# Graph-network kernel on one core: last layer's bias per node, 64 target nodes to a group, a third gate buffer

## What is computed

```python
def _mlp(x, w1, b1, w2, b2, w3, b3):
    x = relu(x @ w1.T + b1)
    x = relu(x @ w2.T + b2)
    return x @ w3.T + b3
def _prop_once(node_states, f_idx, t_idx, edge_features, ...):
    edge_inputs = concatenate([node_states[f_idx], node_states[t_idx], edge_features], axis=1)
    return segment_sum(_mlp(edge_inputs, ...), t_idx)
agg  = _prop_once(x, edge_attr, src, dst, ...)
agg += _prop_once(x, edge_attr, dst, src, ...)
s1 = _gru(x, agg); s2 = _gru(agg, s1); s3 = _gru(s1, s2)
x = layernorm(x + s3)
```

## Time and profile before

| | us |
|---|---|
| median of 3 runs | 2416.49 (2416.43 to 2416.96) |
| profiled execution, its own time | 2414.69 |
| its span in the trace | 2412.9 |
| PE busy | 2290.2 (95%) |
| DVE busy | 1702.4 (71%) |
| ACT busy | 1220.0 (51%) |
| POOL busy | 1356.8 (56%) |

### The profile page before, as it was taken

How to read it: one execution, slowest core, us unless ns; L and a number is a source line. 1 busy time by engine, 2 the same in 40 slices (tenths; PEclk the granted TensorE clock), 3 DMA queues, 4 the chain that set the end, 5 groups by cost and what they waited for, 6 DMA issues and landing times. The chain is left out here.

```text
span 2412.9 us, 42177 instructions
## 1 busy us (share of the span) xinstructions
PE 2290.2 (95%) x12735; PEld 1908.4 (79%) x12735; DVE 1702.4 (71%) x3628; ACT 1220.0 (51%) x2106; POOL 1356.8 (56%) x846
## 2 busy tenths in 40 slices
PE   5999999999999999999999999999999769699997
PEld 3888888888888888888888888888888645488886
DVE  7877878878778788788788788788787456602114
ACT  4555555555556665565565565565555314211112
POOL 2676777777767776776777677777767400000000
PEclk9999999999999999999999999999999979899998
DMA  4456555445555545555545555545555450295863
GB/s 159 83 112 121 98 98 107 89 84 108 96 100 106 92 81 107 94 101 106 93 80 106 95 105 100 97 85 98 100 106 93 60 217 1 107 383 228 348 276 150
DMA packets 233808, 293.73 MB, mean 122 GB/s; under 512 B 125755, under 2 KB 191294, under 8 KB 225228
## 3 DMA queue, kind: packets, MB, share of 16 engines
q1 hardware_dynamic: 160457, 237.91, 35.3%
q0 software_dynamic: 73216, 54.58, 17.7%
HBM read 219.35 MB, written 73.05 MB: 121 GB/s over the span
## 5 line engine op out<-in xcount | busy, mean ns | idle before, releaser
L446 POOL DMA_INDIRECT sums<-outb,target x416 | 684.3, 1645 | 417.3 <-ACT outb L609 167.0
L439 POOL DMA_INDIRECT xg<-in_x,gidx x416 | 667.8, 1605 | 159.5 <-issue 140.2
L591 ACT ACTIVATE h<-ebank,b2c 128x512 f32<-128x512 f32 x416 | 287.3, 691 | 346.6 <-PE ebank L1152 333.2
L1163 PEld LDWEIGHTS ebank<-w3t,h 128*128 128x128 f32 x3328 | 404.1, 192 | 13.8
L1163 PE MATMUL ebank<-w3t,h 128*128 128x128 f32 x3328 | 404.9, 275 | 0.0
L1152 PE MATMUL ebank<-h1h,w2h 128*128 128x512 f32 x832 | 365.3, 439 | 3.9 <-DVE h1l L806 3.9
L1152 PE MATMUL ebank<-h1h,w2l 128*128 128x512 f32 x832 | 329.9, 397 | 0.0
L1152 PE MATMUL ebank<-h1l,w2h 128*128 128x512 f32 x832 | 328.6, 395 | 0.0
L585 ACT ACTIVATE h1h<-hpre 128x512 fp32r<-128x512 f32 x416 | 237.8, 622 | 93.0 <-DVE hpre L801 92.0
L806 DVE SCALAR_TENSOR_TENSOR h1l<-hpre,h1h 128x512 fp32r<-128x512 f32 x416 | 258.4, 678 | 0.0
L1138 PE MATMUL ebank<-sdh,w1h 128*128 128x512 f32 x624 | 247.4, 396 | 2.1 <-DVE sdl L827 1.5
(11 more groups left out here) (254 smaller groups left out, 4000.0 us busy)
## 6 DMA issues: line engine op xcount, KB each, us to landing
ring<-adj SPq DMA_DIRECT2D x54, 1568.0 KB, 8.0
rowb<-along SPq DMA_DIRECT2D x104, 512.0 KB
adj<-band SPq DMA_DIRECT2D x25, 1500.0 KB, 14.6
ef<-in_edge_attr SPq DMA_DIRECT2D x103, 256.0 KB, 2.7
stay<-adj SPq DMA_DIRECT2D x6, 1568.0 KB, 14.4
xg<-in_x,gidx POOLq DMA_INDIRECT x416
sums<-outb,target POOLq DMA_INDIRECT x416
xw<-in_x SPq DMA_DIRECT2D x104, 40.0 KB
```

The lines of the kernel that those rows point to most:

```text
L439: pool.indirect_dma_start(out=to, out_offset=None, in_=a["x"], in_offset=bass.IndirectOffsetOnAxis(ap=ids, axis=0)).then_inc(s_x[par], 16)
L446: pool.indirect_dma_start(out=tables[k % 2], out_offset=bass.IndirectOffsetOnAxis(ap=target[par][:, 1, k:k + 1], axis=0), in_=outb[par][:, ...
L591: nc.scalar.activation(h2[:, way, f, :], bank[6 + f][:, :], ACT.Relu, bias=b2c[:, f:f + 1]).then_inc(s_h2, 1)
L1163: last = nc.tensor.matmul(bank[6 + way][:, t * P:(t + 1) * P], h2[:, way, k, t * P:(t + 1) * P], w3t[:, k, :], start=False, stop=(t == K - ...
```

## The change

**Bias.** `third` loses its two bias products in the path that these inputs take. In place of them the number of edges into each node and out of each is counted, and at the end of the edge stage seven products (2 rows of b3 by 448 nodes' degrees) and seven DVE additions add b3 times the two degrees to `aggt`. The in-degrees come from an accumulated output of `hot` (for each of the window's nodes, the number of the group's edges into it). For the out-degrees the count has 25 more columns, a one-hot of the edge's target block, and DVE adds these columns to `outdeg` in `count_pairs`. At the end both pass through DRAM (two stores, four loads, issued by ACT) to become rows.

**Window.** SPAN is 64 and BACK 10, and `aggt` becomes a slice of a wider `aggw`, so that no window is cut off at the ends; WIN is 19, which makes room for the 25 columns (25 * 19 + 25 = 500).

**Gates** has three buffers, and ACT waits for the cell three back. Beside that, POOL's zero fill at the start of the sum stage waits for the copies into `zt`.

```diff
-WIN = 20
+WIN = 19
 WIDE = NB * WIN
+WIDER = WIDE + NB
-BACK = 16
-SPAN = 80
+BACK = 10
+SPAN = 64
...
@@ ACT, edge stage, the last turn
+                    if win and not ahead:
+                        degrees_away()
                     results(g)
                     sums(g, par, early)
+                    if win and not ahead:
+                        degrees_back()
...
@@ DVE, edge stage
                     nc.vector.tensor_scalar(hot[0:SPAN, :], rowb[par][0:SPAN, 0, :], wnode[0:SPAN, bass.ds(g, 1)], None,
-                                            ALU.is_equal).then_inc(s_hot, 1)
+                                            ALU.is_equal, ALU.add,
+                                            accum_out=indeg[0:SPAN, bass.ds(g + BEFORE, 1)]).then_inc(s_hot, 1)
...
+                    step(nc.vector.tensor_scalar(ints, flat(colkey), 3450.0, None, ALU.mult))
+                    step(nc.vector.tensor_scalar(ints, ints, 16, None, ALU.logical_shift_right))
+                    step(nc.vector.tensor_copy(flat(blkkey), ints))
...
                     for t in range(K):
                         nc.vector.tensor_scalar(rowhot[:, t, :], spots[:, 0:P], of(rowkey, t), None, ALU.is_equal)
-                        last = nc.vector.tensor_scalar(colhot[:, t, :], spots[:, 0:WIDE], of(colkey, t), None, ALU.is_equal)
-                    last.then_inc(s_ah, 1)
+                        nc.vector.tensor_scalar(colhot[:, t, 0:WIDE], spots[:, 0:WIDE], of(colkey, t), None, ALU.is_equal)
+                    nc.vector.tensor_tensor(
+                        colhot[:, :, WIDE:WIDER], column[:, 0:NB].unsqueeze(1).broadcast_to([P, K, NB]),
+                        blkkey[:, bass.ds(g, 1), :].rearrange("p g k -> p (g k)").unsqueeze(2).broadcast_to([P, K, NB]),
+                        ALU.is_equal).then_inc(s_ah, 1)
...
+                    nc.vector.tensor_tensor(outdeg[:, half, :], outdeg[:, half, :], bank[4 + half][:, WIDE:WIDER], ALU.add)
                     nc.vector.tensor_tensor(part, part, bank[4 + half][:, 0:WIDE].rearrange("p (b c) -> p b c", c=WIN),
                                             ALU.add).then_inc(s_acc, 1)
...
+                for n, bk in enumerate((3, 4, 5, 6, 7, 2, 0)):
+                    dve.wait_ge(s_degp, n + 1)
...
+                    nc.vector.tensor_tensor(aggt[:, cols], aggt[:, cols], bank[bk][:, 0:CH], ALU.add).then_inc(s_whole, 1)
...
@@ PE, edge stage
-            def third(g):
+            def third(g, bias=False):
                 pe.wait_ge(s_h2, g * 4 + 4)
                 for way in range(2):
-                    nc.tensor.matmul(bank[6 + way][:, :], ones_r[:, :], b3hl[:, :, :].rearrange("p k d -> p (k d)"),
-                                     start=True, stop=False)
+                    if bias:
+                        nc.tensor.matmul(bank[6 + way][:, :], ones_r[:, :], b3hl[:, :, :].rearrange("p k d -> p (k d)"),
+                                         start=True, stop=False)
...
+                def last_bias():
+
+                    pe.wait_ge(s_degrow, 4 * 16)
+                    pe.wait_ge(s_deg, 2)
+                    pe.wait_ge(s_es, G * 2)
+                    for n, bk in enumerate((3, 4, 5, 6, 7, 2, 0)):
+                        if bk == 0:
+                            pe.wait_ge(s_agg, G)
+                        nc.tensor.matmul(bank[bk][:, 0:CH], b3r[0:2, :], (degree_lo if n < 4 else degree_hi)[0:2, n % 4 * CH:(n % 4 + 1) * CH],
+                                         start=True, stop=True).then_inc(s_degp, 1)
...
@@ GRU stage
-        gates = sb("gates", [P, 2, 2, CH])
+        gates = sb("gates", [P, 3, 2, CH])
...
-                if seq >= 2:
-                    act.wait_ge(s_cell, seq - 1)
+                if seq >= 3:
+                    act.wait_ge(s_cell, seq - 2)
...
@@ POOL, sum stage
+            pool.wait_ge(s_tc, NGR)
             nc.gpsimd.memset(xn[:, :, :], 0.0).then_inc(s_zero, 1)
```

More of the change, by code:

```diff
@@ L58 @@
 PACE = 30
-BACK = 16
-SPAN = 80
-NB_A = 16
+BACK = 10
+SPAN = 64
+NB_A = 19
 AHEAD = 10
-assert G == 4 * ITERS and WIDE <= 512
+assert G == 4 * ITERS and WIDER <= 512
 ADUMMY = NR * AW
@@ L66 @@
 CH = 448
+QS = -(-(N + BACK) // PACE)
+BEFORE = (SPAN - 1) // PACE
+WIDTH_A = (G - 1) * PACE + SPAN
+assert WIDTH_A >= BACK + AW and WIDTH_A % NB_A == 0
 CHUNKS = [(c, min(CH, N - c)) for c in range(0, N, CH)]
@@ L169, in edge_stage @@
         whalf = sd_flat[:, 2 * H:4 * H].rearrange("p (f j c) -> p f j c", f=HB, j=2)
+        degree_lo = hpre[:, :, :, :].rearrange("p f w e -> p (f w e)")
+        degree_hi = sdh[:, :, :].bitcast(fp32).rearrange("p j e -> p (j e)")
         at = lambda t, lo, shape: t[:, lo:lo + int(np.prod(shape))]
@@ L966, in turn, with degrees_out @@
                         places(g + 1, 1 - par, early=early == 2)
+                    if not ahead:
+                        degrees_out()
                     deliver(g)
+                def degrees_out():
+                    dve.wait_ge(s_acc, G * 2)
+                    nc.vector.tensor_tensor(outdeg[:, 2, :], outdeg[:, 0, :], outdeg[:, 1, :], ALU.add).then_inc(s_deg, 1)
+                    dve.wait_ge(s_degT, 1)
+                    nc.vector.tensor_copy(indegs[0:QS, :], bank[2][0:QS, 0:PACE]).then_inc(s_deg, 1)
                 onehot(0, 0, 0)
@@ L1164, in third @@
                                                     h2[:, way, k, t * P:(t + 1) * P], w3t[:, k, :],
-                                                    start=False, stop=(t == K - 1 and k == HB - 1))
+                                                    start=not bias and k == 0,
+                                                    stop=(k == HB - 1 and (not bias or t == K - 1)))
                     last.then_inc(s_l3, 1)
@@ L1193, in pairs_of @@
                         for t in range(2):
-                            last = nc.tensor.matmul(bank[4 + half][:, 0:WIDE], rowhot[:, half * 2 + t, :],
+                            last = nc.tensor.matmul(bank[4 + half][:, 0:WIDER], rowhot[:, half * 2 + t, :],
                                                     colhot[:, half * 2 + t, :], start=(t == 0), stop=(t == 1))
@@ L1241, in turn, with into_each @@
                     total(g, par)
+                def into_each():
+                    pe.wait_ge(s_hot, G)
+                    for j in range(BEFORE + 1):
+                        n = min(PACE, SPAN - j * PACE)
+                        last = nc.tensor.matmul(bank[2][0:QS, 0:n], indeg[0:SPAN, BEFORE - j:BEFORE - j + QS],
+                                                ident[0:SPAN, j * PACE:j * PACE + n], start=(j == 0), stop=(j == BEFORE))
+                    last.then_inc(s_degT, 1)
+                def last_bias():
[7 more added lines that the diff above has]
+                                         start=True, stop=True).then_inc(s_degp, 1)
                 turn_sd(0, 0, 0, start=True)
@@ L1292, in turn @@
                         first(g + 1)
-                    third(g)
+                    third(g, bias=True)
                     total(g, par)
@@ L1899, in gnn_kernel @@
         s_stay = ctx.enter_context(nc.semaphore("s_stay"))
[L1900 to L1901 removed]
+        with nc.sbuf_tensor("aggw", [P, WIDTH_A], fp32) as aggw:
+            edge_stage(nc, a, adj_flat, tables, along, degrees, npairs, aggw, later)
+            aggt = aggw[:, BACK:BACK + AW]
             with nc.sbuf_tensor("stay", [P, TURNS, NB * D], f32r) as stay:
```

59 lines of the change are left out of this document (45 added, 14 removed).

## The result

| | before | after |
|---|---|---|
| median of 4 runs, us | 2416.72 (2416.43 to 2418.67) | 2481.18 (2478.93 to 2482.78) |
| ratio, 95% interval | | 1.0267 (1.0254 to 1.0280) |
| profiled execution, span, us | 2414.69, 2412.9 | 2480.43, 2478.3 |
| median turn, start of L1210 or L1277 to the next, us | 17.88 | 18.43 |

A forecast was written before the change was run, and what follows sets the result against it. PE's own queue, with a second ring through ACT and DVE only 0.2 us behind, bounds the kernel. Terms 24.7 + 3.7 + 1.5 + 1 - 2.7 - 2.3 = +25.9 gave 2442.4 us, range 2400 to 2472.

The forecast's parts named there:

- The ring: PE's L1210, second layer, ACT `sdh`, DVE L830 to `hpre`, ACT `es`, next L1210; to set turns at about 18.17 us.
- DVE's additions, 0.46 us a turn: DVE between L830 and `hpre`: L966, L954 and the accumulated `hot`, less shorter `band` and `colhot`; bounds 0.20 and 0.65.
- the spare: Growth the ring could absorb before PE's turn lengthens: 0.2 us, read from the eight turns with the fold.
- The narrower window ... I take 0: Edge-stage window of 64 nodes in place of 80: columns don't set the pace below 128, so no gain or cost.
- Fold turns, +0.46 in eight: Eight edge-stage turns in which DVE also runs the fold (`wrap`): each grows by the whole 0.46 us, 3.7 in all.
- First turn, end of the edge stage: Three new 416-element steps run once, +1.5 us; the tail of stores, loads, products and additions in DVE's gap, +1.
- Third gate buffer, -2.7: Last layer's ACT sigmoids and last blend can go earlier: -2.7 us, bounds 0 and -3.
- Zero fill, -2.3: POOL's fill moved frees DVE's held `eps` and the path to `zt`: -2.3 us, 0 if adjacency loads bound the start.
- a free accumulated output: Rival, chance 0.14: `hot`'s accumulated output costs DVE nothing, growth 0.20 us a turn, 2415.6 us, no change.
- a shorter ring: Rival, chance 0.14: DVE operations between L830 and `hpre` are held less by POOL; growth under 0.2 us, 2404 us.
- DVE pays more: Rival, chance 0.11: accumulator's second instruction waits, register instruction stalls L967, L954 runs longer; 0.8 us a turn, 2476 us.
- PE alone sets the turn: Rival, chance 0.08: with 0.5 us more spare in the ring, the bias products' whole 54 us come through, 2360 us.

The follow-up runs named there:

- experiment one: Changed kernel with the window back to 80 nodes (SPAN 80, BACK 16, NB_A 10), all else as changed: 2466.45 us, ratio 1.0194.
- experiment ten: Changed kernel with 80 nodes and DVE's order `hpre`, `h1l`, count one-hots, `deliver`, fold, `places`: 2346.49 us, ratio 0.9695.
- Experiments two: Kernel before with the 64-node window alone (SPAN 64, BACK 10): 2446.68 us, ratio 1.0125.
- nine: Changed kernel with its 64-node window, but the two products of `hot` over 80 rows, the 16 added being zeros: 2449.44 us, ratio 1.0123.
- experiment three: Kernel before without the third layer's two bias products, b3 left out of the sums: 2409.19 us, ratio 0.9967.
- experiments seven: Kernel before with DVE's one-hots of the count and `places` moved behind `deliver`: 2441.79 us, ratio 1.0097.
- experiment eleven: Kernel before with DVE's order `hpre`, `h1l`, count one-hots, `deliver`, fold, `places`, and nothing else: 2412.35 us, ratio 0.9974.
- experiment eight: Kernel before with the third gate buffer and POOL's later zero fill alone: 2411.86 us, ratio 0.9972.

## Why the prediction was right and wrong

*The ring, and that it would overtake PE:* right. PE gives up two products and waits for `es` 97 times, 79.5 us, where "some 80 us" was forecast. Two of the signs that were named didn't come: the turn is 18.43 us and not 18.1 to 18.3, and PE's busy time rose by 5 us where it was to fall by 50 or more. The turn is longer by the 64-row products (below), and they make 28 us of PE's busy time: it is 2267.8 us with 80 nodes (experiment one). In experiment ten it is 2237.6, 52.6 less than before.

*DVE's additions, 0.46 us a turn:* right, 0.42 measured. L966 0.09 as said and L954 0.18 for 0.17; `hot` at the slower rate, pitch 0.66, its accumulator read hidden (0.07 had been counted). The place "pitch of `hot` near 0.73" was the one small miss. With 80 nodes the turn grew by 0.27 us where 0.26 was forecast; the spare is 0.13 to 0.15 rather than 0.2.

*"The narrower window ... I take 0":* this is the step that failed, and the largest error of the sum. I priced its columns, and it was its rows that cost. The two products of `hot` went from 80 rows to 64, and PE stands still around them for 0.28 us a turn, some 0.17 ahead of the first, 0.02 between, 0.09 behind: 29 us in 103 turns. Experiments two and nine show it from both sides. The Trainium skill, "TensorEngine Tiling (Array Packing)", section "Key Properties", says that a change of tiling mode drains TensorE, and under "Available Configurations" the page lists 64 rows as a mode of its own; that agrees with the place of the stall, on entry and on exit, and with its absence at 80 rows. That the mode is what changes here is my reading; the runs show only that 64 rows cost it and 80 don't.

*Fold turns, +0.46 in eight:* they are 1.76 us over the median turn in place of 1.38, 0.38 more on top of the 0.27 of every turn. That is 0.65 in place of 0.46, and 5.2 us in place of 3.7. What wasn't in the sum is the clock: PE's wait in a fold turn doubled, from 1.2 to 2.4 us, and half clock followed five times. The five turns behind it are 12.1 us longer together than five median turns, and the long turn at 212 us grew by 1.8; the other turns lie, in sum, 5.6 us further under their median than before, so that about 8 us remain. I had read the earlier trace rows for the wait's length and not asked what a doubled one does.

*First turn, end of the edge stage:* +1.5 and +1.3 for the forecast 1.5 and 1. ACT issues the four loads of the degrees at 1992.80 to 1993.68, PE's first product comes at 1997.21 and its last ends at 2008.03, at half clock; POOL's last addition is under way until 2002.09, and the next stage begins at 2012.88. So the gap hides nearly all.

```profile
1997.21 6.34 PE L1328 MATMUL ebank<-hpre,b3r 2*128 2x448 f32 x8 [10.87 <-DMA sdh<-degrees]
...
2000.54 1.55 POOL L470 DMA_INDIRECT sums<-outb,target  x1 [0.30 <-issue]
...
2012.88 0.17 DVE L1611 MEMSET gones<- 128x128 f32 x1 [4.19 <-PEq L90]
```

*Third gate buffer, -2.7:* the wait behind the last blend fell by 2.6 us, as said; the stage got 4.3 shorter. The rest goes with the clock. In the stage's first 60 us PE is at half clock for 17.9 us before and for 14.9 after. With two buffers the stage takes 147.2 and 147.3 us in experiments two and three, with 15.5 and 16.2 us at half clock there, and 148.2 to 148.4 before and in experiments seven and eleven, with 17.5 to 17.9; with three buffers and 17.5 and 17.6 us of it (experiments one and ten) it takes 145.4. At equal clock the buffer is therefore worth some 3 us. *Zero fill, -2.3:* the sum stage got 0.8 shorter. The nine kernels traced with the later fill take 320.3 to 323.2 us there (mean 321.6), the five without it 322.1 to 323.6 (mean 323.0), so what came is nearer to the lower bound named in the forecast ("0 if the adjacency loads bound that stage's start"), and the held DVE operation wasn't removed but is another one now (experiment eight).

| term, us | forecast | measured |
|---|---|---|
| ring in 95 plain turns | 24.7 | 25.5 (0.268 each) |
| ring in eight fold turns | 3.7 | 5.2 |
| 64-row products | 0 | 28.8 (0.28 by 103) |
| half clock and the other long turns | 0 | 8.1 (the rest of 67.6) |
| first turn, end of the edge stage | 2.5 | 2.8 |
| gates and zero fill | -5.0 | -5.1 |
| sum (the span's growth; the terms are rounded) | 25.9 | 65.4 |

The rivals: a free accumulated output and a shorter ring are refuted by the pitches; "DVE pays more" had nearly the right time for a wrong reason. "PE alone sets the turn" is false for this order and true for that of experiment ten, where the change without its narrower window brings 66 us over the same order without it (experiment eleven). Some 12 of them are the faster first layer and 3 the gates; most of the rest is the bias products, of which the prediction said that PE gets "at most the spare of 0.2 us". Once the ring is short, nearly all of what they cost PE comes through.

## What to carry to other kernels

Price an edit of a tile's size in each dimension of every instruction that it touches, rows as well as columns and partitions; a smaller product can be the slower one, and here 16 rows of zeros bought it back. When a saved instruction stands outside the ring that sets the turn, shorten the ring first, by moving work that nobody waits for soon into the engine's own wait, ahead of the waiting instruction and not behind it. And where a rare long turn makes TensorE wait, ask for the clock behind it too.

## What was unexpected of the hardware

- Two matmuls over 64 rows among matmuls over 128 cost 0.28 us of standing still together; over 80 rows they cost nothing (0.91 to 0.93 us for the stretch in place of 1.19).
- An accumulated output turns the one-tensor comparison of 512 f32 elements from a pitch of 0.47 or less into 0.66 us, and the read of the accumulator costs no pitch.
- In a stage that is otherwise nearly gapless TensorE's clock fell to half behind five of eight waits of 2.4 us and, in experiment three, behind four of eight of 1.5 to 1.8 us; it didn't behind 0.7 us in every turn, nor behind 1.2 us in the fold turns of the kernel before.
- A gather of POOL usually takes about 1 us. In the kernel before, 92 of 416 take 2.6 to 4.2 us, nearly one in each turn; all of them run beside DVE's `h1l` and last until `found` is over (one is 1018.10 + 3.56, with DVE gapless from 1011.81 to 1021.56). In experiments ten and eleven none takes over 1.7 us, and POOL's busy time falls from 1357 to 1102 us in the kernel before with that order. The Trainium skill, "GPSIMD Engine Reference", section "Specifications", names contention with DVE's operations that have two SBUF inputs; `h1l` and `match` are such, and the trace before agrees in time and place. Experiment ten doesn't: 206 of its gathers run beside `h1l` (one at 1016.74 for 1.32 us), and none is held. What else it takes stays open.
- The 18 matmuls of L1138 take 4.20 us before (1011.58 to 1015.78) and those of L1203 4.08 after, 0.233 and 0.227 each. It isn't the bias products, since experiment three keeps 0.233. Every kernel made from the changed one has the shorter pitch, every one made from that before the longer. The cause stays open; the 0.12 us are about the difference between the 0.63 us by which PE's floor fell and the 0.52 counted for the bias products.
